# A decoder layer whose null key and null value leave the inner loop

What is changed: the null key is subtracted from the keys and the null value from the values when the weights are folded, and the first seven tiles' scores take two pairs of accumulator banks by turns, with both halves ahead of the transposes.

## The chip, the core and the metric

The kernel runs on one core of one Trainium2 chip. A core has five engines with queues of their own, which wait for each other by semaphores: TensorE (PE, matrix products, with its weight loads PEld), VectorE (DVE), ScalarE (ACT), GpSimd (POOL) and SyncE (SP, which starts the DMA transfers). PE writes into PSUM, eight banks of 128 partitions by 512 float32 words. The metric is the device time of one execution in microseconds (us), as a median of runs.

## The reference

x has 4 sequences of 1024 rows of 256; the context has 4 times 64 rows of 512. Three blocks, each after a layer norm and each with a residual: a gated recurrence, a cross attention of 16 heads of 64 with one null key and null value, and a feed-forward layer whose activations and weights are rounded to 8 bits and to three values. What matters here:

```
kv = einsum('bmc,cf->bmf', context, Wkv);  k, v = split(kv, 2), heads of 64
k = concatenate((nk, k), axis=-2)          # nk, nv: null_kv[0], null_kv[1], the same for each head
v = concatenate((nv, v), axis=-2)
sim = einsum('bhid,bhjd->bhij', q * DH**-0.5, k)     # 65 scores a head: 64 keys and the null key
attn = softmax(sim, axis=-1)
out = einsum('bhij,bhjd->bhid', attn, v)
out = einsum('bnf,fd->bnd', heads joined, Wout), then layer norm (ln_scale, ln_bias)
```

A softmax doesn't change when the same number is taken from all its scores, and its weights sum to one. So with k - nk as keys the null score is 0 for every row, and with v - nv as values the null value is a constant row added to each output.

## The kernel before

The work is in tiles of 128 rows, 32 in all, and the program is an order written out by hand for each engine, without a planner: what an engine does next is the next call in its function `stages2_3`.

Stage 1 runs the recurrence over eight groups of four tiles and ends about 97 us after the start. Its projections (L1286) multiply float32 operands split into a high and a low part (fp32r), 512 columns at a time.

The fold follows, until about 150 us. It multiplies Wq with the keys (`fold_keys`, L1374, into the maps Mhi and Mlo) and the values with Wout (`fold_values`, L1391, into VW), so that a tile needs only scores = normalised x times map, and output = probabilities times VW. `put_kvT` (ACT, L712) copies the projected context; `put_keys_hi` (ACT, L719) and `put_keys_lo` (DVE, L1030) write the maps' two parts; `put_values_first` (DVE, L1040) and `put_values_second` (ACT, L729) write VW. DVE also forms the null key's map column for each head (`null_key`) and lays the null value 16 times into a selection matrix (`null_values`, L1023), which PE multiplies with Wout in eight accumulating products of float32 (two passes each, L1401), half of them in front of the last `fold_values` and half in step 0.

Stages 2 and 3 are one loop over steps n from -2 to 31. Step n holds on PE: the scores of tile n+2 (`scores_half`, L1270), four groups of 4 heads with 4 x 65 = 260 columns in banks 0 to 3; the transposes of tile n's probabilities (L1510, L1518); the transpose of its null probabilities (L1524, to bank 7); gate and up of the feed-forward layer for tile n-5 (`gate_up`, also L1270; gate in banks 0 and 1, up in 2 and 3, which the scores use too); the output matmuls with VW (L1534, L1539: four float32 products each, two passes a product, so eight in the trace) and with the null values (L1540); in even steps the transposes of the activations of two coming tiles (`pair_T`, L1412); and down for tile n-7.

DVE in step n: `softmax_half` of tile n+2 for each half (maximum L1068, subtraction L1071), the low part of the transposed null probabilities (pTn, L1174), in odd steps xT2lo (L1046), the sum of exponentials of tile n+1 (L1080) and its reciprocal (L1085), gate times up (L1093), its largest value (L1100), the statistics of the output (L1198), the scales (L1132 qs, L1135 qr, L1136 zw, L1104 hw) and the residual (L1152). ACT copies the transposed probabilities (L822, L825, L827), applies silu (L768) and exp (L843), loading a table for each; POOL multiplies the exponentials by the reciprocals (`probabilities`: L554 for the keys, L557 for the null columns).

In steps 0 to 4 (`filling`) there is no gate and up. There the second half of the scores stands behind the transposes on PE, and behind the sum of exponentials and pTn on DVE. A half of the scores waits until the same half of the tile before has been subtracted (`sim_sub`), since all tiles use the same banks.

The functions, with the line numbers of the profile:

## Time and profile before

| | us |
|---|---|
| median of 3 runs | 513.25 |
| lowest, highest | 513.17, 515.15 |
| span of the profiled execution, first to last instruction | 510.8 |
| of it busy: PE, DVE | 476.4, 416.6 |
| of it busy: ACT, POOL | 334.4, 314.1 |

The profile shows one execution. Its own time is the span of 510.8 us, 2.4 less than the median of the runs, which also holds what lies before the first and behind the last instruction. The busy time of PE is a sum over matmuls that overlap each other: how far apart they start tells more than how long one lasts. A line number can be a helper's: L1270 is the helper `group`, under which scores, gate, up, down and the projections of the fold appear; the names of the operands (Mhi, Mlo; wgT; wuT; wdT) tell them apart. A few records of matmuls are missing from the trace, so that a group of four can read x3.

### The profile page before, as it was taken

How to read it: one execution, taken by the hardware profiler on the slowest of the kernel's cores; microseconds unless marked ns; L12 is line 12 of the kernel's file. 1: busy time of each engine (PE TensorE's matmuls, PEld its weight loads, DVE VectorE, ACT ScalarE, POOL GpSimd, SP SyncE). 2: the span in 40 equal slices, each digit the busy share in tenths (PEclk: the TensorE clock that was granted, in tenths of full speed). 3: DMA queues.
4: the chain of work that ended last, by engine and by line, in shares of the span. 5: the costliest groups of instructions: out<-in, count | busy, mean ns of one | idle time of the engine just before them, and what ended most of it. 6: DMA issues, size and time to landing. Idle time of an engine off the chain costs nothing.

```text
span 510.8 us, 8856 instructions
## 1 busy us (share of the span) xinstructions
PE 476.4 (93%) x2934; PEld 390.5 (76%) x2962; DVE 416.6 (82%) x933; ACT 334.4 (65%) x461; POOL 314.1 (61%) x486
## 2 busy tenths in 40 slices
PE   1999999999997998999999999999999999999774
PEld 0778888877676887888888888888888888887432
DVE  4789898968437558799999899898998998997786
ACT  3556652245333334788888888888897888787562
POOL 2234546510003457788787887887878778788861
PEclk9999999999999999999999999999999999999979
DMA  8996000320000000011122211313132212221234
GB/s 256 324 360 255 3 0 1 72 52 2 0 1 1 1 1 7 6 27 42 36 52 45 50 39 38 58 42 49 36 50 46 53 37 52 44 52 37 63 85 117
DMA packets 67116, 31.80 MB, mean 62 GB/s; under 512 B 49664, under 2 KB 65280, under 8 KB 67072
## 3 DMA queue, kind: packets, MB, share of 16 engines
q1 hardware_dynamic: 67072, 31.24, 24.5%
q8 instruction: 24, 0.39, 0.3%
q14 instruction: 20, 0.16, 0.1%
HBM read 15.24 MB, written 4.19 MB: 38 GB/s over the span
## 4 chain that ended last, share of the span: by engine, by line
PE 74%; DVE 11%; POOL 4%; DMA 3%; issue 3%; SPq 2%; ACT 2%; DVEq 0%; POOLq 0%; ACTq 0%
PE psum L1270 33%; PE psum L1534 10%; PE psum L1539 9%; PE psum L1286 9%; DMA xs<-in_x_dram 3%; PE psum L1510 2%; PE psum L1518 2%; SPq L397 2%; PE psum L1412 2%; PE psum L1391 1%; PE psum L1305 1%; DVE den L1080 1%; PE psum L1374 1%; DVE region_d L1071 1%; DVE mx L1068 1%
## 5 line engine op out<-in xcount | busy, mean ns | idle before, releaser
L554 POOL TENSOR_TENSOR region_d<-region_d,rden 128x1024 f32<-128x1024 f32 x32 | 60.9, 1903 | 74.9 <-DVE rden L1085 74.9
L1270 PE MATMUL psum<-Mhi,xT2hi 128*128 128x260 f32 x256 | 75.9, 297 | 0.2
L1270 PE MATMUL psum<-Mlo,xT2hi 128*128 128x260 f32 x256 | 72.9, 285 | 0.0
L1270 PE MATMUL psum<-Mhi,xT2lo 128*128 128x260 f32 x256 | 72.9, 285 | 0.0
L1534 PE MATMUL psum<-VW,region_d 128*128 128x256 f32 x256 | 61.2, 382 | 3.2 <-DVE pTn L1174 3.2
L1539 PE MATMUL psum<-VW,region_d 128*128 128x256 f32 x256 | 60.5, 379 | 0.0
L1534 PEld LDWEIGHTS psum<-VW,region_d 128*128 128x128 f32 x256 | 48.3, 191 | 13.1 <-DVE pTn L1174 4.5
L1068 DVE TENSOR_REDUCE mx<-psum 128x8 f32<-128x520 f32 x64 | 44.5, 696 | 13.0 <-PE psum L1270 11.4
L1539 PEld LDWEIGHTS psum<-VW,region_d 128*128 128x128 f32 x256 | 48.6, 190 | 6.6
L1093 DVE SCALAR_TENSOR_TENSOR region_c<-psum,zw,region_c 128x1024 f32<-128x1024 f32 x32 | 41.0, 1283 | 12.5 <-ACT region_c L768 10.9
L1270 PEld LDWEIGHTS psum<-Mhi,xT2hi 128*128 128x128 f32 x256 | 48.7, 190 | 1.3 <-issue 0.9
L1270 PEld LDWEIGHTS psum<-Mlo,xT2hi 128*128 128x128 f32 x256 | 48.9, 191 | 0.0
L1270 PEld LDWEIGHTS psum<-Mhi,xT2lo 128*128 128x128 f32 x256 | 48.8, 190 | 0.0
L1071 DVE TENSOR_TENSOR region_d<-psum,mx 128x520 f32<-128x520 f32 x64 | 44.8, 699 | 2.2
L843 ACT ACTIVATE region_d<-region_d 128x1040 f32<-128x1040 f32 x32 | 34.3, 1072 | 10.8 <-DVE region_d L1071 10.5
L516 POOL TENSOR_TENSOR pw_out<-pw_in,expo 128x8 f32<-128x8 f32 x8 | 13.2, 1647 | 43.7 <-DVE pw_in L912 43.7
L1100 DVE TENSOR_REDUCE amax<-region_c 128x1 f32<-128x1024 f32 x32 | 39.0, 1219 | 0.9
L1080 DVE TENSOR_REDUCE den<-region_d 128x16 f32<-128x1040 f32 x32 | 39.4, 1230 | 0.4
L768 ACT ACTIVATE region_c<-psum,zw 128x1024 f32<-128x1024 f32 x32 | 35.6, 1114 | 2.7 <-PE psum L1270 2.2
L780 ACT ACTIVATE region_c<-region_c,qr 128x1024 int16<-128x1024 f32 x31 | 35.3, 1139 | 2.8 <-DVE qr L1145 2.4
L571 POOL CAST region_d<-region_c 128x1024 bf16<-128x1024 int16 x31 | 32.2, 1038 | 4.8 <-ACT region_c L780 4.8
L822 ACT ACTIVATE region_d<-psum 128x512 f32<-128x512 f32 x32 | 19.1, 596 | 23.2 <-PE psum L1510 23.2
(151 smaller groups left out, 1217.5 us busy)
## 6 DMA issues: line engine op xcount, KB each, us to landing
out_dram<-xs SPq DMA_DIRECT2D x32, 128.0 KB, 1.9
xs<-in_x_dram SPq DMA_DIRECT2D x1, 2560.0 KB, 13.4
VW<-in_L_xattn_Wkv_dram SPq DMA_DIRECT2D x1, 2048.0 KB, 12.2
region_b<-in_L_xattn_Wkv_dram SPq DMA_DIRECT2D x1, 2048.0 KB, 18.4
xs<-in_x_dram SPq DMA_DIRECT2D x3, 512.0 KB, 7.4
region_w<-in_L_ffn_w_gate_dram SPq DMA_DIRECT2D x2, 512.0 KB, 10.3
region_w<-in_L_ffn_w_up_dram SPq DMA_DIRECT2D x2, 512.0 KB, 7.7
region_w<-in_L_ffn_w_down_dram SPq DMA_DIRECT2D x8, 128.0 KB, 5.1
```

The lines of the kernel that those rows point to most:

```text
L554: pool.tensor_tensor(p2[:, v, 0:H * MK].rearrange("p (h j) -> p h j", j=MK), e[:, :, 0:MK], rden[:, v, :].unsqueeze(2).broadcast_to([P, H, ...
L768: act.activation(hid3[v], banks(0, 2).rearrange("p b n -> p (b n)"), ACT.Silu, scale=zw[:, (n - 5) % 4, 0:1]).then_inc(silu_ready, 1)
L780: act.activation(nq3, hid3[t % 2], ACT.Copy, scale=qr[:, t % 2, 0:1]).then_inc(hq_done, 1)
L1068: dve.tensor_reduce(mx[:, hh, :].rearrange("p (b h) -> p b h", h=HB), scores, AX.X, ALU.max) \
L1071: dve.tensor_tensor(e2[:, u, hh * 2 * HB * J:(hh + 1) * 2 * HB * J].rearrange("p (b h j) -> p b h j", b=2, j=J), scores, mx[:, hh, :].rear ...
L1080: dve.tensor_reduce(den[:, :], e2[:, slot, :].rearrange("p (h j) -> p h j", j=J), AX.X, ALU.add) \
L1093: dve.scalar_tensor_tensor(out=hid3[v], in0=banks(2, 2).rearrange("p b n -> p (b n)"), scalar=zw[:, (n - 5) % 4, 1:2], in1=hid3[v], op0=AL ...
L1100: dve.tensor_reduce(amax[:, v, 0:1], hid3[v], AX.X, ALU.max, apply_absolute_value=True) \
L1270: mm = pe.matmul(dst, lhsT, rhs, start=i == 0, stop=i == len(terms) - 1)
L1286: mm = pe.matmul(bank(b), lhsT, rhs, start=i == 0, stop=i == len(terms) - 1)
L1534: pe.matmul(bank(7, D), pT[:, pair, :], VW[:, batch(n), pair, :], start=pair == 0, stop=False)
L1539: pe.matmul(bank(7, D), pT[:, pair, :], VW[:, batch(n), pair, :], start=False, stop=False)
```

## The change

The null key and value are loaded as two columns and negated once on POOL; `put_kvT` adds the negated column as a bias, so that maps and VW are made of k - nk and v - nv. The maps have 64 columns a head instead of 65, and a half of the scores is 8 heads of 64, one group of 512 columns in one bank. On DVE each half gets a third operation between maximum and subtraction: the shift -max(maximum, 0) of each head, written to the place of the null score in the row of exponentials (whose score is 0), and the subtraction becomes an addition of it. The transpose, the copy, the low part and the probabilities of the null columns go. The null value enters as one product of 33 rows (`ones_r` with `vnull`, the null value times Wout summed over the heads, in two parts), first in the output's accumulation; POOL sums Wout over its eight pieces for it, and DVE writes its low part in step 0 behind the second half of softmax of tile 2.

Scores of tile t lie in banks 2 (t % 2) and the next for t below 7, then always in 0 and 1; gate moves to banks 2 and 3, up to 0 and 1. In every step both halves stand ahead of the transposes, and each half of up waits for one half of softmax. The semaphores and buffers not shown are renamed or dropped to match.

```diff
@@ -362,9 +357,9 @@
-        def filling(n):
-            return isinstance(n, int) and 0 <= n < 5
+        def score_bank(t, hh):
+            return 2 * (t % 2) + hh if t < 7 else hh
@@ -524,14 +520,24 @@
+                    pool.wait_ge(null_loaded, 64)
+                    pool.tensor_scalar(nulls_neg[:, :], nulls[:, :], -1.0, 0.0, ALU.mult, ALU.add) \
+                        .then_inc(nulls_negated, 1)
...
+            pool.wait_ge(nvsel_zero, 1)
+            for row in (0, NR - 1):
+                pool.tensor_copy(nvsel[:, row:row + 1], nulls[:, 1:2]).then_inc(nv_set, 1)
+            pool.wait_ge(wout_loaded, 16)
...
-            pool.memset(nvsel, 0.0).then_inc(nvsel_zero, 1)
+            pool.tensor_tensor(wsum, wout[:, 0, :], wout[:, 1, :], ALU.add).then_inc(wout_summed, 1)
+            for pair in range(2, HC):
+                pool.wait_ge(wout_summed, pair - 1)
+                pool.tensor_tensor(wsum, wsum, wout[:, pair, :], ALU.add).then_inc(wout_summed, 1)
@@ -551,12 +557,8 @@
-                pool.tensor_tensor(p2[:, v, 0:H * MK].rearrange("p (h j) -> p h j", j=MK), e[:, :, 0:MK],
+                pool.tensor_tensor(p2[:, v, :].rearrange("p (h j) -> p h j", j=MK), e[:, :, 0:MK],
...
-                    .then_inc(p_ready, 1)
-                pool.tensor_tensor(p2[:, v, H * MK:].rearrange("p (m h) -> p m h", h=H),
-                                   e[:, :, MK].unsqueeze(1).broadcast_to([P, NP // H, H]),
-                                   rden[:, v, :].unsqueeze(1).broadcast_to([P, NP // H, H]), ALU.mult) \
@@ -709,13 +711,15 @@
-                act.activation(kvT[:, i % 4, :], bank(i % 2, BM), ACT.Copy).then_inc(kvT_ready, 1)
+                null = 0 if i < HC else 1
+                act.activation(kvT[:, i % 4, :], bank(i % 2, BM), ACT.Identity, bias=nulls_neg[:, null:null + 1]) \
+                    .then_inc(kvT_ready, 1)
...
-                    at = slot_of(2 * i + half_) * J
+                    at = slot_of(2 * i + half_) * MK
@@ -991,41 +993,10 @@
-            def null_key(k):
...
-                dve.tensor_scalar(hi, null, DH ** -0.5, None, ALU.mult).then_inc(mnull_hi, 1)
-                dve.scalar_tensor_tensor(out=lo, in0=null, scalar=DH ** -0.5, in1=hi.bitcast(F32), op0=ALU.mult,
-                                         op1=ALU.subtract).then_inc(mnull_put, 1)
-            def null_values():
-                for pair in range(HC):
-                    for j in range(2):
-                        rows = slice(j * DH, (j + 1) * DH)
-                        column = nvsel[rows, :].rearrange("p (c m h) -> p c m h", c=HC, h=H)[:, pair, 0::2, slot_of(2 * pair + j)]
-                        dve.tensor_copy(column, nv[rows, :].broadcast_to([DH, 3])).then_inc(nv_set, 1)
...
-                    at = slot_of(2 * i + half_) * J
+                    at = slot_of(2 * i + half_) * MK
@@ -1060,19 +1027,18 @@
-                scores = banks(2 * hh, 2)[:, :, 0:HB * J].rearrange("p b (h j) -> p b h j", j=J)
+                scores = bank(score_bank(n, hh)).rearrange("p (h j) -> p h j", j=MK)
+                e = e2[:, u, hh * HB * J:(hh + 1) * HB * J].rearrange("p (h j) -> p h j", j=J)
...
-                    if positive(2 * n - 2):
-                        dve.wait_ge(p_ready, 2 * n - 2)
-                dve.tensor_reduce(mx[:, hh, :].rearrange("p (b h) -> p b h", h=HB), scores, AX.X, ALU.max) \
-                    .then_inc(max_done, 1)
+                    if positive(n - 1):
+                        dve.wait_ge(p_ready, n - 1)
+                dve.tensor_reduce(mx[:, hh, :], scores, AX.X, ALU.max).then_inc(max_done, 1)
...
-                dve.tensor_tensor(
-                    e2[:, u, hh * 2 * HB * J:(hh + 1) * 2 * HB * J].rearrange("p (b h j) -> p b h j", b=2, j=J),
-                    scores,
-                    mx[:, hh, :].rearrange("p (b h) -> p b h", h=HB).unsqueeze(3).broadcast_to([P, 2, HB, J]),
-                    ALU.subtract).then_inc(sim_sub, 1)
+                dve.tensor_scalar(e[:, :, MK], mx[:, hh, :], 0.0, -1.0, ALU.max, ALU.mult).then_inc(shift_done, 1)
+                dve.wait_ge(shift_done, 2 * n + hh + 1)
+                dve.tensor_tensor(e[:, :, 0:MK], scores, e[:, :, MK].unsqueeze(2).broadcast_to([P, HB, MK]), ALU.add) \
+                    .then_inc(sim_sub, 1)
@@ -1161,20 +1127,12 @@
-                if exists(n + 2, T) and not filling(n):
+                if exists(n + 2, T):
...
-                    dve.wait_ge(vwn_hi, 1)
-                    lo = VWnull[4 * H:NP, :]
-                    dve.tensor_tensor(lo, psum[4 * H:NP, 7, 0:D], lo.bitcast(F32), ALU.subtract).then_inc(vwn_ready, 1)
-                if exists(n, T):
-                    dve.wait_ge(pTn_hi, n + 1)
-                    lo = pTn[2 * H:3 * H, :]
-                    dve.tensor_tensor(lo, psum[2 * H:3 * H, 7, D:D + P], lo.bitcast(F32), ALU.subtract) \
-                        .then_inc(pTn_ready, 1)
-                if filling(n):
-                    softmax_half(n + 2, 1, u)
+                    dve.wait_ge(vnull_hi, 1)
+                    lo = vnull[NR - 1:NR, :]
+                    dve.tensor_tensor(lo, psum[NR - 1:NR, 7, 0:D], lo.bitcast(F32), ALU.subtract).then_inc(vnull_ready, 1)
@@ -1394,13 +1352,11 @@
-            def null_values(first, end):
-                pe.wait_ge(nv_set, 2 * HC)
-                for pair in range(first, end):
-                    mm = pe.matmul(psum[0:NP, 7, 0:D], nvsel[:, pair * NP:(pair + 1) * NP], wout[:, pair, :],
-                                   start=pair == 0, stop=pair == HC - 1)
-                return mm
+            def null_values():
+                pe.wait_ge(nv_set, 2)
+                pe.wait_ge(wout_summed, HC - 1)
+                pe.matmul(psum[0:NR, 7, 0:D], nvsel[:, :], wsum, start=True, stop=True).then_inc(vnull_psum, 1)
@@ -1444,22 +1398,21 @@
-                if n == 0 and hh == 1:
+                if n == 1:
...
-                if positive(2 * n - 1 + hh):
+                if n >= 7:
...
+                elif n >= 2:
+                    pe.wait_ge(sim_sub, 2 * n - 3 + hh)
...
-                    pe.wait_ge((silu_ready, h_ready)[hh], n - 7)
-                for g in (2 * hh, 2 * hh + 1):
-                    mm = group(bank(g, HB * J),
-                               [(xT[:, (u4 // 2) % 2, k, (u4 % 2) * P:(u4 % 2 + 1) * P],
-                                 m[:, k, b, g * HB * J:(g + 1) * HB * J])
-                                for k in range(KD) for xT, m in ((xT2hi, Mhi), (xT2hi, Mlo), (xT2lo, Mhi))])
-                mm.then_inc(sim_psum, 1)
+                    pe.wait_ge(h_ready, n - 7)
+                group(bank(score_bank(n, hh)), [(xT[:, (u4 // 2) % 2, k, (u4 % 2) * P:(u4 % 2 + 1) * P],
+                                  m[:, k, b, hh * HB * MK:(hh + 1) * HB * MK])
+                                 for k in range(KD) for xT, m in ((xT2hi, Mhi), (xT2hi, Mlo), (xT2lo, Mhi))]) \
+                    .then_inc(sim_psum, 1)
...
@@ -1475,19 +1428,18 @@
-                pe.wait_ge(sim_sub, upto(2 * n + 5, 2 * T))
...
-                    mm = group(bank(j), [(nT3[:, slot, k, :], wgT[:, k, j * 512:(j + 1) * 512]) for k in range(KD)])
+                    mm = group(bank(2 + j), [(nT3[:, slot, k, :], wgT[:, k, j * 512:(j + 1) * 512]) for k in range(KD)])
...
-                pe.wait_ge(sim_sub, upto(2 * n + 6, 2 * T))
...
-                    mm = group(bank(2 + j), [(nT3[:, slot, k, :], wuT[:, k, j * 512:(j + 1) * 512]) for k in range(KD)])
+                    pe.wait_ge(sim_sub, upto(2 * n + 5 + j, 2 * T))
+                    mm = group(bank(j), [(nT3[:, slot, k, :], wuT[:, k, j * 512:(j + 1) * 512]) for k in range(KD)])
@@ -1496,14 +1448,13 @@
                     if n == 0:
-                        null_values(HC // 2, HC).then_inc(vwn_psum, 1)
-                    if not filling(n):
-                        scores_half(n + 2, 1, (u4 + 2) % 4, half(n + 2 - u), batch(n + 2))
+                        null_values()
+                    scores_half(n + 2, 1, (u4 + 2) % 4, half(n + 2 - u), batch(n + 2))
                 else:
...
-                    pe.wait_ge(p_ready, 2 * n + 2)
+                    pe.wait_ge(p_ready, n + 1)
                     if positive(n):
@@ -1517,27 +1468,25 @@
                     mm.then_inc(pT1_psum, 1)
+                if exists(n + 2, T) and exists(n - 5, T):
+                    gate_up(n, v)
+                if exists(n, T):
                     if positive(n):
...
                     if n == 0:
-                        pe.wait_ge(vwn_ready, 1)
-                    pe.transpose(psum[0:NP, 7, D:D + P], p2[:, u, H * MK:], ident[:, :]).then_inc(pTn_psum, 1)
-                if filling(n):
-                    scores_half(n + 2, 1, (u4 + 2) % 4, half(n + 2 - u), batch(n + 2))
-                if exists(n + 2, T) and exists(n - 5, T):
-                    gate_up(n, v)
-                if exists(n, T):
-                    pe.wait_ge(pTn_ready, n + 1)
+                        pe.wait_ge(vnull_ready, 1)
+                    pe.matmul(bank(7, D), ones_r[:, :], vnull[:, :], start=True, stop=False)
                     pe.wait_ge(pT0_ready, n + 1)
                     for pair in range(HC // 2):
-                        pe.matmul(bank(7, D), pT[:, pair, :], VW[:, batch(n), pair, :], start=pair == 0, stop=False)
+                        pe.matmul(bank(7, D), pT[:, pair, :], VW[:, batch(n), pair, :], start=False, stop=False)
                 if exists(n, T):
...
                     for pair in range(HC // 2, HC):
-                        pe.matmul(bank(7, D), pT[:, pair, :], VW[:, batch(n), pair, :], start=False, stop=False)
-                    pe.matmul(bank(7, D), pTn[:, :], VWnull[:, :], start=False, stop=True).then_inc(out_psum, 1)
+                        mm = pe.matmul(bank(7, D), pT[:, pair, :], VW[:, batch(n), pair, :], start=False,
+                                       stop=pair == HC - 1)
+                    mm.then_inc(out_psum, 1)
                 if u == 0 and exists(n, T - 4):
...
                 if exists(n - 7, T):
```

On DVE, the odd step of the steady part, before. mx holds the maxima, region_d the rows of exponentials (and xT2lo's source), and den the sums:

```order
L1068 TENSOR_REDUCE mx<-psum 128x8 [waits p_ready,sim_psum]
L1071 TENSOR_TENSOR region_d<-psum,mx 128x520 [waits max_done]
L1068 TENSOR_REDUCE mx<-psum 128x8 [waits sim_psum]
L1071 TENSOR_TENSOR region_d<-psum,mx 128x520 [waits max_done]
L1174 TENSOR_TENSOR pTn<-psum,pTn 16x128 [waits pTn_hi]
L1046 TENSOR_TENSOR xT2lo<-psum,xT2hi 128x512 [waits xT2_ready]
L1080 TENSOR_REDUCE den<-region_d 128x16 [waits exp_done]
```

The same place after:

```order
L1036 TENSOR_REDUCE mx<-psum 128x8 [waits p_ready,sim_psum]
L1038 TENSOR_SCALAR region_d<-mx 128x8 [waits max_done]
L1040 TENSOR_TENSOR region_d<-psum,region_d 128x8x64 [waits shift_done]
L1036 TENSOR_REDUCE mx<-psum 128x8 [waits sim_psum]
L1038 TENSOR_SCALAR region_d<-mx 128x8 [waits max_done]
L1040 TENSOR_TENSOR region_d<-psum,region_d 128x8x64 [waits shift_done]
L1017 TENSOR_TENSOR xT2lo<-psum,xT2hi 128x512 [waits xT2_ready]
L1046 TENSOR_REDUCE den<-region_d 128x16 [waits exp_done]
```

Two small operations have come in, each in a chain of waits, and the one on pTn has gone. The neighbours stand as they did.

On PE, a step among 0 to 4, before; the first row opens the first half of the scores, and the one that waits for sim_sub behind the null transpose (80x128) opens the second:

```order
L1270 MATMUL psum<-Mhi,xT2hi 128x260 [waits sim_sub,xT2_lo_ready]
...
L1510 MATMUL psum<-ident,region_d 128x128 [waits pT0_ready,p_ready]
L1510 MATMUL psum<-ident,region_d 128x128 x3
L1518 MATMUL psum<-ident,region_d 128x128 [waits pT1_ready]
L1518 MATMUL psum<-ident,region_d 128x128 x3
L1524 MATMUL psum<-ident,region_d 80x128 [waits y2_ready]
L1270 MATMUL psum<-Mhi,xT2hi 128x260 [waits sim_sub,xT2_lo_ready]
...
L1534 MATMUL psum<-VW,region_d 128x256 [waits pT0_ready,pTn_ready]
```

And after, from the start of the second half of the scores:

```order
L1228 MATMUL psum<-Mhi,xT2hi 128x512 [waits sim_sub,xT2_lo_ready]
...
L1461 MATMUL psum<-ident,region_d 128x128 [waits pT0_ready,p_ready]
L1461 MATMUL psum<-ident,region_d 128x128 x3
L1469 MATMUL psum<-ident,region_d 128x128 [waits pT1_ready]
L1469 MATMUL psum<-ident,region_d 128x128 x3
L1479 MATMUL psum<-vnull,ones_r 128x256 [waits y2_ready]
L1482 MATMUL psum<-VW,region_d 128x256 [waits pT0_ready]
```

The second half has moved in front of the transposes, where the wait for sim_sub is one for the tile two before. Between the transposes and VW nothing is left but the null product, and VW no longer waits for pTn.

## Rows read from the trace of the kernel before

**Rows 1.** The page: its span, and the chain that ended last, by engine.
```profile
span 510.8 us, 8856 instructions
...
PE 74%; DVE 11%; POOL 4%; DMA 3%; issue 3%; SPq 2%; ACT 2%; DVEq 0%; POOLq 0%; ACTq 0%
```

**Rows 2.** Chain in order of time: start, length (us), work; steady part.
```profile
241.19 1.73 PE psum L1534 x8
...
448.65 1.73 PE psum L1534 x8
```

**Rows 3.** Timeline of PE, steady step: start, length (us), line, operands, shape.
```profile
308.33 0.37 PE L1270 MATMUL psum<-Mhi,xT2hi 128*128 128x260 f32 x1
...
311.30 0.60 PE L1510 MATMUL psum<-ident,region_d 128*128 128x128 f32 x4
...
313.14 1.03 PE L1270 MATMUL psum<-wuT,region_d 128*128 128x512 bf16 x4
314.01 1.89 PE L1534 MATMUL psum<-VW,region_d 128*128 128x256 f32 x8
```

**Rows 4.** Timeline of DVE, the same step and the next; brackets: idle before.
```profile
310.06 0.70 DVE L1068 TENSOR_REDUCE mx<-psum 128x8 f32<-128x520 f32 x1 [0.51 <-PE psum L1270]
...
312.96 0.28 DVE L1174 TENSOR_TENSOR pTn<-psum,pTn 16x128 fp32r<-16x128 f32 x1
313.28 0.69 DVE L1046 TENSOR_TENSOR xT2lo<-psum,xT2hi 128x512 fp32r<-128x512 f32 x1
...
319.23 0.17 DVE L1132 TENSOR_SCALAR qs<-amax 128x2 f32<-128x2 f32 x1
319.43 0.17 DVE L1135 RECIPROCAL qr<-qs 128x2 f32<-128x2 f32 x1
319.51 0.21 DVE L1136 TENSOR_SCALAR zw<-wscale,qs 128x2 f32<-128x2 f32 x1
...
320.15 0.69 DVE L1068 TENSOR_REDUCE mx<-psum 128x8 f32<-128x520 f32 x1
...
325.86 1.28 DVE L1093 SCALAR_TENSOR_TENSOR region_c<-psum,zw,region_c 128x1024 f32<-128x1024 f32 x1 [0.73 <-ACT region_c L768]
```

**Rows 5.** Chain in order of time, steps 0 to 4.
```profile
167.32 1.82 PE psum L1534 x8
...
171.43 1.44 PE psum L1270 x12
174.33 1.15 DVE den L1080
...
202.20 1.99 PE psum L1534 x8
```

**Rows 6.** Timeline of PE, VW of step 1.
```profile
176.12 1.99 PE L1534 MATMUL psum<-VW,region_d 128*128 128x256 f32 x8 [0.66 <-DVE pTn L1174]
```

**Rows 7.** Chain, a stretch of the projections of stage 1.
```profile
38.82 4.12 PE psum L1286 x18
```

**Rows 8.** Timeline of PE, first and last fold of values.
```profile
131.61 1.96 PE L1391 MATMUL psum<-region_b 64*64 64x256 f32 x32 [1.17 <-DVE Mlo L1030]
...
148.66 1.96 PE L1391 MATMUL psum<-region_b 64*64 64x256 f32 x32
```

**Rows 9.** Timeline of ACT, in front of the last fold.
```profile
147.32 1.08 ACT L729 ACTIVATE VW<-psum 128x512 f32<-128x512 f32 x2
```

**Rows 10.** Timeline of POOL, its first work behind the fold.
```profile
158.56 1.90 POOL L554 TENSOR_TENSOR region_d<-region_d,rden 128x1024 f32<-128x1024 f32 x1 [50.72 <-DVE rden L1085]
```

**Rows 11.** Busy by window: length, PE, PEld, DVE, ACT, POOL; clock, DMA, GB/s.
```profile
164.00:165.00 1.00, 0.72 (x4) 0.72 (x5) 0.23 (x1) 0.24 (x2) 1.00 (x1) 0.50 0.00 0
```

**Rows 12.** Timeline of PE, the null transpose of step 0.
```profile
164.28 0.43 PE L1524 MATMUL psum<-ident,region_d 128*80 128x128 f32 x1 [2.32 <-DVE VWnull L1169]
```

**Rows 13.** Timeline of ACT, copy of the first four transposes, steady step.
```profile
311.94 0.60 ACT L822 ACTIVATE region_d<-psum 128x512 f32<-128x512 f32 x1 [0.76 <-PE psum L1510]
```

**Rows 14.** All executions of L1132: ns shortest/median/longest, first and last start.
```profile
L1132 DVE TENSOR_SCALAR qs<-amax x32: 153/169/172, 198.5 to 492.8; 128x2 f32<-128x2 f32 x26, 128x1 f32<-128x1 f32 x6
```

98 lines of the change are left out of this document (34 added, 64 removed).

## The prediction, made before the changed kernel ran

> **What bounds the kernel now.** I read the page first: the chain that ended last lies for 74% on PE and for 11% on DVE [rows 1]. Then the chain in order of time, which gives the pace: the matmuls of probabilities times VW start at 241.19 for one tile and at 448.65 twenty tiles later [rows 2], so a tile costs 10.37 us and a pair of tiles 20.75. Tiles go in pairs because an even step also transposes two coming tiles' activations on PE, and an odd step subtracts their rounded part on DVE (L1046).
>
> Next PE's timeline in one such step [rows 3]. From the scores at 308.33 to the transposes at 311.30 are 2.97 us; to up at 313.14 another 1.84, which are gate (as long as up, 0.87) and nine transposes of 0.108; up 0.87; then VW, twice 1.73. There is no hole: PE is full. DVE's timeline [rows 4] is nearly as full. From 310.06 to 320.15 it never waits, 10.09 us; in the next step it waits 0.73 us for the silu. So two limits stand side by side: PE's own work, and a loop through DVE: first maximum of the odd step, all its work up to the next step's first maximum, two halves of softmax, and then PE's up, VW and the rest until the next scores. A gain on PE is therefore not simply passed on.
>
> Before that come five steps without the feed-forward part, where no engine is full: VW starts at 167.32 and, four steps on, at 202.20 [rows 5], 8.72 us a step. There the order decides, and VW waits for DVE's pTn, 0.66 us at 176.12 [rows 6], which stands behind the sum of the exponentials (174.33 [rows 5]).
>
> **The change part by part.**
>
> *Scores, steady.* Before: 24 matmuls of 260 columns, 0.12 us apart (12 in 1.44 [rows 5]), 2.9 us and a start-up of 0.07. After: 12 of 512 columns. The nearest row has the same kind of operands in the first stage, 18 in 4.12 us [rows 7], 0.229 each, so 2.75. Bounds: 0.217, the pace of the four bf16 matmuls of 512 columns (313.14 to 314.01 [rows 3]), and 0.24, two of 260. I take 0.229: 0.17 us a tile less on PE. The null transpose goes too, 0.11. The null product of 80 rows is replaced by one of 33 rows with as many columns: even. PE alone then needs 20.75 - 2 x 0.28 = 20.2 us a pair.
>
> *DVE, steady.* Each half gains one tensor_scalar of 128x8 between maximum and subtraction, each waiting for the one before. Its nearest row is qs, a tensor_scalar of 128x2 with a dependent successor: 0.17 long, and 0.20 from its start (319.23) to the next start [rows 4]. So +0.40 a tile. The subtraction on pTn goes, 0.32 (312.96 to 313.28). 520 elements become 512, about 0.01 for each pass. Net +0.06 to 0.08 a tile. But of the stretch that up waits for, maximum to last subtraction, all 0.40 count: 2.90 (310.06 to 312.96) becomes 3.27. Bounds of one shift: 0.08, the distance of two small operations that don't wait for each other (qr and zw, 319.43 and 319.51), and 0.32, the place of pTn's subtraction. Eased is what up waits for: its second half alone needs the second half of softmax.
>
> *The loop.* First maximum of an odd step until that of the next: 10.09 + 0.40 - 0.32 = 10.17. Then 3.27 until the last subtraction. Then PE: the second half of up 0.43, null product 0.11, VW 3.46, transposes 0.43, down 0.87 (eight of 256 columns, as many as up's), in all 5.3; then 1.65 until the first half of the next scores has been written (before 310.06 - 308.33 = 1.73, by eleven gaps of 0.12 and a last matmul of 0.28; now five of 0.229 and a last one of some 0.4). Sum 20.4, and with about 0.1 for the restart of PE after a wait 20.5. That is above PE's 20.2, so the loop binds: 20.75 - 20.5 = 0.25 a pair. Eleven pairs (steps 8 to 29): **-2.8**.
>
> *Fold.* The 16 small copies of null_values on DVE go. PE waited 1.17 us in front of the first fold of values for the subtraction behind them [rows 8]; 0.1 of it I leave, since ACT's last copy for that fold may then be late: 1.05. The eight null passes of 0.216 before the last fold (148.66 [rows 8]) go from PE, but that fold also needs ACT's two copies from 147.32, 1.08 long [rows 9], done at 148.40: worth 0.15. The two null_key blocks on DVE never held PE up: nothing. POOL's seven new additions fall where it idled for 50.72 us until 158.56 [rows 10]: nothing; without that cover the null value's product would wait for them. Together -1.2: scores start at 149.4 (before 148.66 + 1.9 = 150.6).
>
> *First tiles.* PE now can write three tiles' scores in a row, so from 151.05 (149.4 + 1.65) DVE alone sets the pace: six halves of 1.64 (3.27/2), two sums with reciprocal of 1.45 (from 174.33 [rows 5] until pTn's 0.32 in front of VW at 176.12), 0.35 waiting for POOL's first probabilities (two tiles share the buffers), 0.42 for the low part of the null value, on which tile 0's output waits: 164.5. VW starts at 164.8 instead of 167.3. But the clock: from 164 to 165 PE had the granted clock 0.50 [rows 11], 1.2 GHz instead of 2.4, after a wait of 2.32 us for DVE [rows 12]. After the change PE waits longer there (160.3 to 164.5), and what follows is VW, the longest group. If the low clock lasts as long as before, some 3.4 us until VW's start, that costs 1.7 us. So tile 0 is done only **-0.9** earlier (2.5 less 1.7, fold included).
> [...]
>
> *Steps 1 to 4.* Both halves of the scores run ahead of the transposes (2.8), then 1.3 until ACT has copied the first four (0.64 from the transposes' start at 311.30 to the copy at 311.94, and 0.60 [rows 13]), null product and VW 3.57: 7.7 us, and 8.15 with two coming tiles' transposes, mean 7.9. DVE has 6 to 6.6 us of work in such a step and no longer stands in front of VW. 4 x (8.72 - 7.9) = **-3.3**.
>
> *Steps 5 to 7* begin the feed-forward part; DVE's extra work and PE's smaller 0.28 about cancel: **-0.1**. *Drain:* two steps in which pTn (0.3) is off DVE's path: **-0.6**; the rest is unchanged, gate and up only trade banks.
>
> **Sum.** -0.9 - 3.3 - 0.1 - 2.8 - 0.6 = -7.7 against the profiled execution's span of 510.8 [rows 1], so 503.1. The median of the runs lies 2.4 above that span: 505.5.
>
> **The rivals.**
> 1. *PE alone binds, the loop is shorter.* If a shift costs 0.12, the loop falls to 20.2 and so does a pair: 11 x 0.55 = 6.1 instead of 2.8: 502.2. For it: PE shows hardly a wait today. Against: 10.09 us of DVE without a hole.
> 2. *The steady part gives nothing.* A shift of 0.26 eats the 0.25 of a pair: 508.3. For it: a strided result, 65 elements apart, of which before shows no small one.
> 3. *The clock does not fall, or falls on nothing:* 1.7 less, 503.8.
> 4. *The change doesn't do in steps 1 to 4 what it says.* If scores ahead only push the transposes back, and VW starts no earlier (another wait, for y2 or the probabilities, in pTn's place), 3.3 are lost: 508.8. For it: no engine is full there, so waits decide. Against: what VW waits for by name is pTn [rows 6].
> 5. *Slower.* The shift stands in the loop four times a pair. Before it decides, the whole gain must be eaten: 4 x 11 x (x - 0.2) = 7.7, so x = 0.38 us. At 0.55 the kernel takes 505.5 + 15.4 = 521. It would need the shift to wait for POOL's running operation. Against it: qs, of the same kind, took 153 to 172 ns in all its 32 executions [rows 14].
> The Trainium skill (GPSIMD Engine Reference, Key points) has just this rule: POOL shares its SBUF interfaces with VectorE and contends with DVE instructions in a 2-port mode or with two SBUF inputs. By it the shift, with its one source and its result in SBUF, could be such an instruction, and this rival's 521 its price; the 32 executions of qs do not bear it out.
>
> **How the numbers follow.** Forecast 0.44, first rival 0.17, second 0.15, third 0.08, fourth 0.09, fifth 0.04, and 0.03 for something unseen near no change. The likeliest one's own range is 503.5 to 507.5. A shift at its upper bound, 0.32, gives 505.5 + 11 x 0.48 = 510.8, one at its lower and scores at 0.217 give PE's limit 20.0 a pair and 500.2. Over all cases I give 500.5 to 509.8. Under 0.5% (2.6 us) this kernel's measurement can't tell a difference: faster means below 510.7. Faster 0.87, same 0.08, slower 0.05.
>
> **What would show it.** In the profile after: score matmuls 0.229 apart; pairs of 20.5 us between VW starts, with PE waiting shortly for DVE's subtraction in front of the second half of up in every other step, and DVE without idle time from an odd step's first maximum to the next; shifts of 0.17, 0.20 apart from what follows; steps 1 to 4 of 7.7 and 8.15 us without a wait for DVE in front of VW; VW of tile 0 at 164.8 and a granted clock of 0.5 around it. Wrong, if DVE waits for PE in every step of the steady part (then rival 1), if shifts last over 0.25 (rival 2 or 5), or if the low clock spreads into steps 1 to 4.

## The result, and the profile after

The changed kernel takes **522.5 us** (median of 4 runs, 522.31 to 525.78) against 513.59 for the kernel before in the same session: ratio 1.0172, 95% interval 1.0139 to 1.0206. It is slower by 1.7%, where 505.5 us had been forecast. Two executions lie far outside the rest, 817.39 us for the kernel before beside the first group of runs and 1223.74 for the kernel with the null value early; no ratio counts them, and the latter kernel's median is 496.16 without it. The profiled execution:

```profile
span 520.7 us, 7943 instructions
...
PE 72%; DVE 14%; DMA 4%; SPq 3%; issue 2%; POOL 2%; ACT 2%; POOLq 0%; ACTq 0%; DVEq 0%
```

Against [rows 1], the share of DVE in the chain has gone up from 11 to 14%. Where the 9.9 us of span arose is seen best in the starts of the matmuls of probabilities times VW (PE's timeline; L1534 before, L1482 after), in us:

| step | 0 | 1 | 4 | 7 | 29 | 31 | end |
|---|---|---|---|---|---|---|---|
| before | 167.12 | 176.12 | 202.20 | 230.95 | 458.56 | 475.54 | 510.8 |
| after | 167.03 | 177.36 | 201.18 | 230.11 | 465.73 | 481.74 | 520.7 |
| after less before | -0.1 | +1.2 | -1.0 | -0.8 | +7.2 | +6.2 | +9.9 |

So the steady part (steps 7 to 29, eleven pairs) lost 8.0, the drain behind step 31 another 3.7, and the first steps gained 0.8 where 4.3 had been forecast. A steady pair takes 21.55 us in place of 20.75.

PE's timeline in an odd steady step, the one to hold against [rows 3]:

```profile
310.01 0.48 PE L1228 MATMUL psum<-Mhi,xT2hi 128*128 128x512 f32 x1
310.32 0.39 PE L1228 MATMUL psum<-Mlo,xT2hi 128*128 128x512 f32 x1
310.55 0.40 PE L1228 MATMUL psum<-Mhi,xT2lo 128*128 128x512 f32 x1
...
312.84 0.60 PE L1461 MATMUL psum<-ident,region_d 128*128 128x128 f32 x4
313.28 0.60 PE L1469 MATMUL psum<-ident,region_d 128*128 128x128 f32 x4
313.71 1.03 PE L1228 MATMUL psum<-wgT,region_d 128*128 128x512 bf16 x4
314.58 0.59 PE L1228 MATMUL psum<-wuT,region_d 128*128 128x512 bf16 x2
315.55 0.61 PE L1228 MATMUL psum<-wuT,region_d 128*128 128x512 bf16 x2 [0.38 <-DVE region_d L1040]
316.09 0.38 PE L1479 MATMUL psum<-vnull,ones_r 33*128 33x256 f32 x1
316.40 1.99 PE L1482 MATMUL psum<-VW,region_d 128*128 128x256 f32 x8
318.23 1.89 PE L1487 MATMUL psum<-VW,region_d 128*128 128x256 f32 x8
319.96 1.04 PE L1228 MATMUL psum<-wdT,region_d 128*128 128x256 bf16 x8
```

The scores take 2.83 us (2.97 before), the matmuls 0.23 apart as forecast but for 0.31 behind the first. The transposes take 0.87. Up now has a hole in its middle: its second half starts 0.97 behind its first and not 0.43, since PE waits for DVE's subtraction. Then the null product: from its start to down's are 3.87 us, where VW and the null product before took 3.57 (376.21 to 379.78 in the trace of before). That is 0.3 more for a part that I had called even.

DVE's shifts (L1038) in that step, and what POOL does then:

```profile
312.40 0.37 DVE L1038 TENSOR_SCALAR region_d<-mx 128x8 f32<-128x8 f32 x1
...
314.13 0.64 DVE L1038 TENSOR_SCALAR region_d<-mx 128x8 f32<-128x8 f32 x1
```
```profile
312.26 0.48 POOL L603 TENSOR_SCALAR region_d<-region_d,qr 128x256 f32<-128x256 f32 x1
...
314.01 0.73 POOL L549 TENSOR_TENSOR region_d<-region_d,lb_bc 128x256 f32<-128x256 f32 x1
```

The first shift ends at 312.77, POOL's instruction at 312.74; the second at 314.77 and POOL's at 314.74. That a running instruction of POOL keeps the shift from ending is called a hold in what follows. In the first steps it is POOL's probabilities, its longest instruction there:

```profile
158.10 1.50 DVE L1038 TENSOR_SCALAR region_d<-mx 128x8 f32<-128x8 f32 x1
```
```profile
157.67 1.91 POOL L560 TENSOR_TENSOR region_d<-region_d,rden 128x1024 f32<-128x1024 f32 x1 [44.58 <-DVE rden L1051]
```

All 64 shifts, put beside POOL's timeline: 36 began while such an instruction ran, one of them only 0.02 us behind its start, and all 36 ended 0.02 to 0.04 us after it. Four more began when less than 0.14 us of one was left, eight under POOL's instructions of 128x1 and sixteen beside nothing; these took 0.17 to 0.20. Four of the eight had over 0.3 us of a 128x1 power (0.57 long) still ahead of them. One of these four:

```profile
387.25 0.17 DVE L1038 TENSOR_SCALAR region_d<-mx 128x8 f32<-128x8 f32 x1
```
```profile
387.00 0.57 POOL L583 TENSOR_TENSOR sc<-sc,expo 128x1 f32<-128x1 f32 x1
```

In sum the 64 last 26.5 us, undisturbed they would last 64 x 0.175 = 11.2.

Tile 0, which answers to [rows 11, 12]:

```profile
166.53 0.58 PE L1479 MATMUL psum<-vnull,ones_r 33*128 33x256 f32 x1 [5.81 <-DVE vnull L1135]
167.03 3.78 PE L1482 MATMUL psum<-VW,region_d 128*128 128x256 f32 x8
```
```profile
164.00:165.00 1.00, 0.00 (x0) 0.00 (x0) 1.00 (x1) 0.00 (x0) 1.00 (x1) 0.91 0.00 0
165.00:171.00 6.00, 4.47 (x10) 3.48 (x11) 1.41 (x3) 0.00 (x0) 0.27 (x1) 0.50 0.01 3
171.00:172.00 1.00, 1.00 (x5) 0.82 (x4) 0.00 (x0) 0.00 (x0) 0.00 (x0) 0.67 0.00 0
```

PE waited 5.81 us in front of it. Within this wait, at about 164.8, its granted clock fell to 0.50 (1.2 GHz of 2.4) and stayed there until about 171.7: some 6.8 us, 5.1 of them with PE at work. Before, it was some 3.4 us (0.98 in 163 to 164, 0.50 until 167, 0.81 in 167 to 168), 3.1 of them at work.

### The profile page after: what moved, and what is told of

The parts are those of the page before. It is cut to its first block, busy times and chain, and to the rows that moved or that the text cites. A ratio compares the mean times of both kernels' runs of the same rounds, so it can differ in the third digit from the quotient of the medians.

```text
span 520.7 us, 7943 instructions
## 1 busy us (share of the span) xinstructions
PE 481.2 (92%) x2532; PEld 362.8 (70%) x2532; DVE 420.7 (81%) x939; ACT 329.3 (63%) x429; POOL 308.2 (59%) x465
## 4 chain that ended last, share of the span: by engine, by line
PE 72%; DVE 14%; DMA 4%; SPq 3%; issue 2%; POOL 2%; ACT 2%; POOLq 0%; ACTq 0%; DVEq 0%
PE psum L1228 30%; PE psum L1482 11%; PE psum L1487 10%; PE psum L1244 9%; DVE region_d L1040 4%; DVE mx L1036 3%; DVE region_d L1038 3%; DMA xs<-in_x_dram 3%; PE psum L1479 2%; SPq L392 2%; PE psum L1332 2%; PE psum L1461 2%; PE psum L1469 2%; PE psum L1349 1%; PE psum L1263 1%
## 5 line engine op out<-in xcount | busy, mean ns | idle before, releaser
L1482 PE MATMUL psum<-VW,region_d 128*128 128x256 f32 x256 | 65.6, 400 | 0.1
L1487 PE MATMUL psum<-VW,region_d 128*128 128x256 f32 x256 | 61.0, 381 | 0.0
L1036 DVE TENSOR_REDUCE mx<-psum 128x8 f32<-128x512 f32 x64 | 43.5, 680 | 14.2 <-PE psum L1228 14.2
L1482 PEld LDWEIGHTS psum<-VW,region_d 128*128 128x128 f32 x256 | 47.1, 194 | 9.7 <-ACT region_d L826 0.3
L1228 PE MATMUL psum<-Mhi,xT2hi 128*128 128x512 f32 x128 | 53.1, 415 | 0.3 <-DVE xT2lo L1017 0.3
L1228 PE MATMUL psum<-Mhi,xT2lo 128*128 128x512 f32 x128 | 50.3, 393 | 0.0
L1228 PE MATMUL psum<-Mlo,xT2hi 128*128 128x512 f32 x128 | 49.9, 390 | 0.0
L1040 DVE TENSOR_TENSOR region_d<-psum,region_d 128x512 f32<-128x512 f32 x64 | 44.3, 692 | 2.2
L1228 PE MATMUL psum<-wuT,region_d 128*128 128x512 bf16 x128 | 36.4, 381 | 3.6 <-DVE region_d L1040 3.4
L1228 PE MATMUL psum<-wgT,region_d 128*128 128x512 bf16 x128 | 33.7, 387 | 4.6 <-DMA region_d<-region_c 4.6
L784 ACT ACTIVATE region_c<-region_c,qr 128x1024 int16<-128x1024 f32 x31 | 35.3, 1140 | 3.4 <-DVE qr L1111 2.9
L1244 PE MATMUL psum<-xT1hi,w1hi 128*128 128x512 f32 x96 | 32.1, 416 | 1.9 <-ACT xT1hi L674 1.2
```

What stands on the lines that cost most here:

```text
L784: act.activation(nq3, hid3[t % 2], ACT.Copy, scale=qr[:, t % 2, 0:1]).then_inc(hq_done, 1)
L1036: dve.tensor_reduce(mx[:, hh, :], scores, AX.X, ALU.max).then_inc(max_done, 1)
L1040: dve.tensor_tensor(e[:, :, 0:MK], scores, e[:, :, MK].unsqueeze(2).broadcast_to([P, HB, MK]), ALU.add) \
L1228: mm = pe.matmul(dst, lhsT, rhs, start=i == 0, stop=i == len(terms) - 1)
L1244: mm = pe.matmul(bank(b), lhsT, rhs, start=i == 0, stop=i == len(terms) - 1)
L1482: pe.matmul(bank(7, D), pT[:, pair, :], VW[:, batch(n), pair, :], start=False, stop=False)
```

## The experiments

Four groups. Times are medians; each ratio is to the kernel before on the same chip.

**1. The shift, and the place of the null product.**

> The changed kernel with the null product behind the eight pairs of VW instead of ahead of them. Theory B (the null product ahead costs PE 0.3 us in every tile, and PE is what binds): 0.3 x 32 = 9.6 less, 513. Theory A (the shifts' hold on DVE binds, and the null product lies in the loop only once a pair): 0.3 x 12 = 3.6 less, 519. If its place is free: 522.5.

```
-  pe.matmul(bank(7, D), ones_r, vnull, start=True, stop=False)
   ... 16 matmuls of VW ...
+  pe.matmul(bank(7, D), ones_r, vnull, start=False, stop=True).then_inc(out_psum, 1)
```

522.43 us, ratio 1.0135 (1.0102 to 1.0168): nothing gained. A steady pair fell by 0.2 (21.36), and steps 1 to 4, where the product ahead lies beside the wait for ACT's copy, took 25.85 instead of 23.82. Theory B in this form (its place costs) falls. The 0.3 us are there in both places: with the product last, the stretch from VW's start to what follows it takes 3.86 us in an odd step, against 3.57 before.

> The changed kernel without the shift: the maximum is written negated into the null column by the reduction itself, and the subtraction adds it (the clamp of the maximum at zero is left out). Theory A: the hold of the shifts goes from the loop (a median of 0.37 us four times a pair), a pair falls from 21.5 to PE's own 20.7 with the null product ahead, and the first tile comes 2.5 us earlier: 11 x 0.85 + 1.5, so 511 to 512. Theory B alone: at most the 0.2 of an undisturbed shift counts, 519 or more.

```
-  dve.tensor_reduce(mx[:, hh, :], scores, AX.X, ALU.max)
-  dve.tensor_scalar(e[:, :, MK], mx[:, hh, :], 0.0, -1.0, ALU.max, ALU.mult)
+  dve.tensor_reduce(e[:, :, MK], scores, AX.X, ALU.max, negate=True)
```

This leaves out the clamp of the maximum at zero, as every kernel without the shift does here. 510.27 us, ratio 0.9898 (0.9855 to 0.9942): 12 us from this edit, as theory A has it.

> Both edits, no shift and the null product last. Both theories together: PE alone sets the pace, 20.2 us a pair by 20.7 less 0.5: 505 to 507, faster than the kernel before. If only one of the two mattered, this equals that one's time.

```
   the edits of the last two kernels together
```

511.72 us, ratio 0.9929 (0.9899 to 0.9959). The expected 505 to 507 was missed: without the shift PE binds at 20.7 to 20.8 us a pair, wherever the null product stands. So PE had gained nothing from the change, though its scores and transposes had become 0.25 a tile shorter. That opened the second question below.

> The changed kernel with the shift in the same place, of the same operands and with the same waits, but as a reduction over one element that writes the negated value, instead of a tensor_scalar (clamp at zero left out). Theory A with the form of the instruction as its cause: the hold by POOL is gone, the shift lasts 0.1 to 0.2 in all cases, and the kernel takes 514 to 517. Rival: POOL's work holds any DVE instruction that reads and writes SBUF, then its times spread from 0.17 to 1.5 as now and the kernel stays at 522.5.

```
-  dve.tensor_scalar(e[:, :, MK], mx[:, hh, :], 0.0, -1.0, ALU.max, ALU.mult)
+  dve.tensor_reduce(e[:, :, MK], mx[:, hh, :].unsqueeze(2), AX.X, ALU.max, negate=True)
```

512.04 us, ratio 0.9953 (0.9922 to 0.9984). One instruction in the same place, with the same operands and waits, but of another form (and without the clamp). All executions of L1038, first of the changed kernel, then of this one (ns shortest/median/longest):

```profile
L1038 DVE TENSOR_SCALAR region_d<-mx x64: 174/370/1500, 152.1 to 463.6; 128x8 f32<-128x8 f32 x64
```
```profile
L1038 DVE TENSOR_REDUCE region_d<-mx x64: 167/168/171, 152.6 to 454.2; 128x8 f32<-128x8 f32 x64
```

One of them under POOL's probabilities:

```profile
158.51 0.17 DVE L1038 TENSOR_REDUCE region_d<-mx 128x8 f32<-128x8 f32 x1
```
```profile
158.07 1.91 POOL L560 TENSOR_TENSOR region_d<-region_d,rden 128x1024 f32<-128x1024 f32 x1 [44.57 <-DVE rden L1051]
```

25 of the 64 reductions began with over 0.3 us left of an instruction of POOL larger than 128x1, and all of them took 0.17. So the form of the instruction decides, and 10 of the 17 us between forecast and result hang on it.

**2. The rows of the null product.** PE's weight loads in the changed kernel (the engine's second row in the profile; they normally run beside the matmul ahead):

```profile
315.55 0.11 PEld L1228 LDWEIGHTS psum<-wuT,region_d 128*128 128x128 bf16 x2 [0.87 <-DVE region_d L1040]
316.09 0.18 PEld L1479 LDWEIGHTS psum<-vnull,ones_r 33*128 33x128 f32 x1 [0.42 <-issue]
316.40 1.59 PEld L1482 LDWEIGHTS psum<-VW,region_d 128*128 128x128 f32 x8
```

The load of the 33-row product starts when up's last matmul is about through, and VW's first load (316.40) when the null product is. Both are bare, that is, no matmul runs beside them. Hence theory C: it is the number of rows.

> The changed kernel without the shift, and with the null product of 128 rows instead of 33 (the 95 new rows of the null value are zero, so nothing changes in what is computed). Theory C: a product of 33 rows between products of 128 costs PE 0.40 to 0.49 us instead of 0.11, since its weights are not loaded beside the matmul ahead. Then a pair falls from 20.8 to 20.2 us and the time by 12 x 0.6 and 0.3 for each of the first steps: 501 to 503. Rival D: the null product costs that much because vnull and ones_r are read where before had pTn, whatever the rows: no change, 510.

```
-  NR = DH // 2 + 1
+  LO, NR = DH // 2, 128          # the low part stays in row 32
```

500.25 us, ratio 0.9745 (0.9713 to 0.9778). A steady pair is 20.17. The same place of it, loads and matmuls:

```profile
324.31 0.75 PEld L1226 LDWEIGHTS psum<-wuT,region_d 128*128 128x128 bf16 x4
325.17 0.19 PEld L1477 LDWEIGHTS psum<-vnull,ones_r 128*128 128x128 f32 x1
325.39 1.60 PEld L1480 LDWEIGHTS psum<-VW,region_d 128*128 128x128 f32 x8
```
```profile
324.52 1.03 PE L1226 MATMUL psum<-wuT,region_d 128*128 128x512 bf16 x4
325.20 0.47 PE L1477 MATMUL psum<-vnull,ones_r 128*128 128x256 f32 x1
325.50 1.67 PE L1480 MATMUL psum<-VW,region_d 128*128 128x256 f32 x7
```

(A record of VW is missing there; the other steps show x8 and the same distance.) From up's start to VW's are 0.98 us, of which up is 0.87: the null product costs 0.11, what the forecast took. In the kernel with 33 rows and no wait it was 1.27 (380.90 to 382.17 with no shift): 0.40.

> The same with 80 rows, as many as the null product of the kernel before has. Theory C, since before showed 0.11 for it: as with 128 rows, 501 to 503. Rival D: 510.

```
-  LO, NR = DH // 2, 128
+  LO, NR = DH // 2, 80
```

501.33 us, ratio 0.976 (0.9727 to 0.9792); a pair 20.18.

> The same with 64 rows. If theory C holds and it is the number of 32-row strips that must be that of the neighbours (rounded up to two, three or four), 64 behaves like 33: 510. If only a count that is no multiple of 32 costs: like 128 rows, 501 to 503.

```
-  LO, NR = DH // 2, 128
+  LO, NR = DH // 2, 64
```

510.84 us, ratio 0.9936 (0.9916 to 0.9956); a pair 20.82.

> No shift, with the null product of 32 rows (high and low part in rows 31 and 0, the same sum). Theory C: anything that doesn't fill more than 64 rows is loaded apart from its neighbours, 510. Rival: only 33 to 64 rows are, and 32 load like 128: 500.

```
-  LO, NR = DH // 2, 128          # high part in row 0, low part in row 32
+  LO, NR = DH // 2, 32           # high part in row 31, low part in row 0
```

509.52 us, ratio 0.9909 (0.9874 to 0.9945); a pair 20.81. So 32, 33 and 64 rows cost one price, and 80 and 128 the other. The step lies between 64 and 80 rows; nothing in between was tried.

> The changed kernel as it is, shift included, with 128 rows in the null product. The DVE loop with the held shifts binds a pair at 21.55; the null product lies in that loop once a pair: 12 x 0.3 and 1 for the first steps, 517 to 519. If PE's 0.3 a tile counted in full beside the held shifts: 513.

```
-  NR = DH // 2 + 1
+  LO, NR = DH // 2, 128          # the shift stays as changed
```

506.21 us, ratio 0.9872 (0.9828 to 0.9917), less than both values expected: the held loop does not bind at 21.55, a pair is 20.17. The profiled execution is the longest of the four, 509.94, and its first scores start at 152.54, some 3 us later than in the others of the changed kernel and its variants. All its shifts:

```profile
L1038 DVE TENSOR_SCALAR region_d<-mx x64: 174/176/1497, 155.0 to 452.4; 128x8 f32<-128x8 f32 x64
```

The median is 176, the undisturbed length. 16 of the 64 last over 0.2 us, where 36 did with 33 rows, and in sum they last 18.6 us instead of 26.5: the order on both engines is the same, but with steps 0.3 us shorter most shifts no longer fall on what holds them. The two causes are not a sum:

| | 33 rows | 128 rows |
|---|---|---|
| shift as changed | 522.5 (1.0172) | 506.2 (0.9872) |
| no shift | 510.3 (0.9898) | 500.25 (0.9745) |

> Without the shift, 128 rows, and the null product last. With the rows right, its place is worth nothing in the steady part (PE has the same work); tile 0 needs the null value either way. 500 to 501. If the place has a price of its own beside the rows, over 1 us from the 500.25 of the kernel with it ahead.

```
   no shift, 128 rows, and the null product behind VW, as in the first experiment
```

502.96 us, ratio 0.977 (0.975 to 0.979), where 500 to 501 had been expected: 2.7 above the kernel with the product ahead, though the two ratios' intervals overlap. A pair is 20.17 as there. It starts tile 0 at 163.54 instead of 163.91 and is 0.4 behind by step 31 (462.26 against 461.89), lost in steps 1 to 4; the rest lies in the drain.

**3. Both causes in the kernel before, and the length of POOL's instruction.**

> The kernel before with its null product cut from 80 rows to 64 (the last 16 rows, the low part's, are left out of it). Theory C: the weights of the product are no longer loaded beside the matmul ahead, nor those of the next beside it, 0.3 a tile on a PE that is full: 514 + 30 x 0.3 = 521 to 524. Rival: the price belongs to ones_r and vnull in the changed kernel and not to the rows: 514.

```
-  pe.matmul(bank(7, D), pTn[:, :], VWnull[:, :], start=False, stop=True)
+  pe.matmul(bank(7, D), pTn[0:64, :], VWnull[0:64, :], start=False, stop=True)
```

It leaves the low part's last 16 rows out. 521.66 us, ratio 1.0131 (1.0108 to 1.0155), for less work. A pair went from 20.75 to 21.17. One of its loads:

```profile
374.34 0.18 PEld L1540 LDWEIGHTS psum<-VWnull,pTn 64*128 64x128 f32 x1 [0.33 <-issue]
```

> The kernel before with a tensor_scalar of 128x8 between each maximum and its subtraction, which only copies the maximum. Undisturbed (0.20 from its start to the next): at most 0.8 a pair less the 0.73 that DVE waits: 514 to 518. Theory A, held by POOL, whose two instructions for the probabilities run some 2.2 us a tile: a mean of 0.4 and a maximum of 1.5 or more, 520 to 528.

```
+  dve.tensor_scalar(mx_copy[:, hh, :], mx[:, hh, :], 1.0, 0.0, ALU.mult, ALU.add)
   dve.tensor_tensor(e2[...], scores, mx_copy[...], ALU.subtract)    # was mx
```

523.48 us, ratio 1.0163 (1.0145 to 1.0181). All its copies of the maximum:

```profile
L1073 DVE TENSOR_SCALAR mx_copy<-mx x64: 171/172/1486, 152.9 to 464.1; 128x8 f32<-128x8 f32 x64
```

23 of the 64 last over 0.2 us. So the hold needs nothing of the rest of the change, nor the strided result. Pairs are 21.0 in most of the steady part and 21.7 in three, and this shows a limit of the hold. In an odd step the first copy begins just behind the start of POOL's tensor_scalar of 128x256. In the three long pairs it begins 0.06 to 0.08 us behind it and is held; in seven others 0.03 to 0.05 behind it, and is not. One of each kind, DVE's row and then POOL's:

```profile
334.73 0.44 DVE L1073 TENSOR_SCALAR mx_copy<-mx 128x8 f32<-128x8 f32 x1
```
```profile
334.66 0.48 POOL L603 TENSOR_SCALAR region_d<-region_d,qr 128x256 f32<-128x256 f32 x1
```
```profile
313.72 0.17 DVE L1073 TENSOR_SCALAR mx_copy<-mx 128x8 f32<-128x8 f32 x1
```
```profile
313.68 0.48 POOL L603 TENSOR_SCALAR region_d<-region_d,qr 128x256 f32<-128x256 f32 x1
```

Why the early ones escape isn't shown; POOL's instruction is not longer for it.

> The changed kernel with POOL's probabilities of a tile as four instructions of 256 elements instead of one of 1024. Theory A (a shift is held until the instruction that runs on POOL has ended, 1.9 us for one of 1024, about 0.5 for one of 256): the longest shift falls from 1.50 to 0.7 or less, and the time to 514 to 518. Rival: it is held until POOL's whole work for the tile is done, or by something else: shifts up to 1.5 as before and 522 or, by four starts instead of one on POOL, more.

```
+  for c in range(4):       # heads 4c to 4c+3 of the probabilities
       pool.tensor_tensor(p2[...][:, hs, :], e[:, hs, 0:MK], rden[...], ALU.mult)
```

521.74 us, ratio 1.0133 (1.0115 to 1.0152). The mechanism came as expected, the time did not:

```profile
L1040 DVE TENSOR_SCALAR region_d<-mx x64: 174/360/760, 151.6 to 464.4; 128x8 f32<-128x8 f32 x64
```

The longest shift is halved: 0.76, now under an addition of 128x256, and 0.59 under one of the four pieces. Step 7 starts at 227.77 instead of 230.11. But in the steady part it is POOL's other instructions that hold the shifts, its four pieces take 2.33 us and not 1.90, and a pair is 21.82.

**4. The first steps.**

> No shift, 128 rows, but the scores of all tiles in one pair of banks, so that PE waits with a tile's first half for the last tile's subtraction. By the forecast the two pairs of banks were worth 0.9 at tile 0 and most of the 3.3 us of steps 1 to 4: 503 to 504. Rival: the order of the two halves ahead of the transposes does it alone, and the second pair is worth under 1 us: 500 to 501.

```
-  return 2 * (t % 2) + hh if t < 7 else hh
+  return hh
```

501.64 us, ratio 0.9764 (0.9732 to 0.9796). VW starts at 163.85, 173.49, 196.73 and 224.58 in steps 0, 1, 4 and 7; with two pairs of banks it is 163.91, 173.55, 196.79 and 224.67. In this kernel, without the shift and with 128 rows, the second pair brings nothing; the 1.3 us by which its profiled execution is longer lie behind step 31.

> No shift, 128 rows, and the null value's product, copy and low part one step earlier, so that the low part (0.42 on DVE) stands in front of tile 2's softmax and not behind it. In the kernel with 128 rows PE stood idle for 3.58 us before tile 0's output, waiting for it, and then ran at half clock. Theory: VW(0) starts when ACT has copied the first probabilities, 160.3 instead of 163.9, the clock stays high, and the whole kernel gains 3 to 5 us: 495.5 to 497.5. Rival: later steps are set by DVE's order, which the edit doesn't shorten, and the lead is given back: 499 to 500.5.

```
 PE:   if n == -1: null_values(); scores_half(n + 2, 0, ...)    # was n == 0, behind it
 ACT:  if n == -1: copy of vnull                                 # was n == 0
 DVE:  if n == 0: low part of vnull; softmax_half(n + 2, 0, u)   # was behind both halves
```

**496.39 us, ratio 0.9647 (0.9618 to 0.9676)**: the fastest kernel of this study, 3.5% below before.

> The kernel with the null value early once more, for its profile: PE without the wait of 3.58 us before tile 0's output, VW(0) at 160.3, the granted clock at 1.0 from there, and steps of 7.6 to 8.1 behind it.

```
   no edit against the last kernel
```

496.91 us in one execution. PE at tile 0, and its clock behind it:

```profile
159.85 0.66 PE L1459 MATMUL psum<-ident,region_d 128*128 128x128 f32 x4 [0.89 <-POOL region_d L560]
...
160.70 0.36 PE L1477 MATMUL psum<-vnull,ones_r 128*128 128x256 f32 x1
161.19 1.99 PE L1480 MATMUL psum<-VW,region_d 128*128 128x256 f32 x8
```
```profile
161.00:171.00 10.00, 9.74 (x50) 8.30 (x50) 7.70 (x14) 4.90 (x10) 6.19 (x8) 1.00 0.01 2
```

No wait for the null value, no fall of the clock: VW(0) comes at 161.19 (160.3 had been expected), 2.7 us earlier than with the null value late and VW(1) 4.3 earlier (169.22 against 173.55), and this lead is kept to step 31 (457.47 against 461.89). Of 4.3 us, 2.7 are the wait and 1.6 the clock: with the null value late the clock was 0.50 for some 3.4 us behind VW(0), and half of that is 1.7.

> The changed kernel, shift included, with 128 rows and the null value's work one step earlier. If the shift costs only what holds it (two holds of 1.5 us in the first steps, undisturbed later, as with 128 rows alone), it lies 3 to 6 us above the 496.4 of the same kernel without it: 500 to 502, and the whole gain of the early null value is there beside the shift, against 506.2.

```
+  dve.tensor_scalar(e[:, :, MK], mx[:, hh, :], 0.0, -1.0, ALU.max, ALU.mult)    # the shift again
```

498.94 us, ratio 0.9728 (0.9673 to 0.9782): below what was expected. With rows and wait mended the shift costs 2.5 us by the medians (4 by the ratios), where it cost 12 (14) in the changed kernel.

## Why the prediction was wrong, by its steps

**DVE, steady: "+0.40 a tile", bounds 0.08 to 0.32 for one shift.** Wrong in kind. A shift lasts 0.17 or, in most cases, as long as POOL's instruction still runs, up to 1.50: 0.41 on average. Its upper bound came from the nearest small instruction and left out a wait. The fifth rival had the right mechanism, at a chance of 0.04. That it also had the right time ("At 0.55 the kernel takes [...] 521") is luck: by its own formula the measured 0.41 gives some 515, and the null product makes up the rest. What kept it there were the 32 executions of qs [rows 14], and they were no test: 17 began with POOL idle and 14 under one of its 128x1 instructions, 11 of them just as it ended. Only one (481.15, 0.15 long, under the cast below) began under a larger one, and it has a single element. Two rows of before could have told; zw is of the same form, 0.21 long in its 31 other executions, and ended here with POOL's cast:

```profile
481.42 0.32 DVE L1136 TENSOR_SCALAR zw<-wscale,qs 128x2 f32<-128x2 f32 x1
```
```profile
480.69 1.04 POOL L571 CAST region_d<-region_c 128x1024 bf16<-128x1024 int16 x1
```

What tells is the longest time of every instruction of this form on DVE, beside POOL's timeline. 29 of the other executions of zw ran under a 128x1 power and were not held, as the four shifts.

The Trainium skill says it outright on a page that I had not used (SBUF — State Buffer, SBUF: two separate sides): the port pair of VectorE and GpSimd is an exclusive lock, and whoever has it keeps it for the whole instruction. These traces agree: ends 0.02 to 0.04 us behind POOL's, 36 times. By the Trainium skill (VectorE: DVE Perf Modes, Mode 2×_2P) the mode in which one fp32 tensor with source and result in SBUF takes both ports is for tensor_scalar and tensor_copy; that the reduction in the shift's place was never held fits this. Neither section has the exceptions seen here, POOL's 128x1 powers and the copies that began right behind POOL's tensor_scalar.

**"The null product of 80 rows is replaced by one of 33 rows with as many columns: even."** Wrong by 0.3 us a tile, and the costliest single step: mending it alone gives 506.2. That this is near the forecast's 505.5 is in part luck: its pairs are 0.3 shorter than forecast, and its first steps some 3 us behind. I had priced the matmul by its columns, and not the two weight loads at its sides. It sits on PE, which is full, in every step. With it mended a pair is 20.17, the 20.2 that the forecast gave PE alone (first rival); the loop of 20.5, which I had put above it, does not bind even with the shift in it, so that sum was 0.3 too high.
The Trainium skill (TensorE: Matmul & The Clock Gate, Part 3) says in its list of what overlaps that a weight load does so with a matmul only where their row groups differ, though it also names a background weight buffer that a load can go to. The traces differ from the list: loads of 80 and 128 rows overlapped with matmuls of 128 rows, and loads of 32 to 64 rows, which need only part of the rows, did not. The measurement decides.

**Tile 0: "-0.9".** VW(0) was due at 164.8 and came at 167.03. Two held shifts (158.10 and 163.87) add 2.6 us on DVE's way there. The low clock then lasted some 6.8 us and not 3.4: VW of step 1 comes 10.33 us behind VW(0), and 8.03 where the clock stays at 1.00 (null value early), so it costs 2.3 us and not 1.7. With 128 rows and no shift, where PE waits 3.58 us, it costs 1.6, as forecast; the term was right for the wait that I had foreseen and too small for the one that the holds made. With 128 rows and no shift VW(0) is at 163.9, a little better than forecast.

**Steps 1 to 4: "7.7 us, and 8.15".** Right from step 1 on, where the starts are 8.17, 8.04 and 7.61 apart. But the first of the four steps took 10.33, mostly for the low clock, so that the four gained 0.9 and not 3.3. That the second pair of banks makes this possible, as the text has it ("PE now can write three tiles' scores in a row"), is not so: it brings nothing. What does was not undone by itself; the order of the halves, pTn's absence or both remain.

**Fold: "-1.2".** Scores start at 149.7, forecast 149.4 (149.1 to 150.2 in nearly all profiles of the variants). ACT's copies with a bias take 0.47 instead of 0.38; whether they are the 0.3 isn't shown.

**Drain: "-0.6".** Steps 30 and 31 gained 1.0, but what follows step 31 took 39.0 us instead of 35.3. In the profiles here it lies between 35.3 and 39.1, without regard to the edits, and the longer ones have a low clock at the very end. First before, then after:

```profile
505.00:510.00 5.00, 2.33 (x21) 1.49 (x18) 1.39 (x3) 0.60 (x1) 0.00 (x0) 1.00 0.23 79
```
```profile
515.00:521.00 6.00, 2.20 (x10) 1.02 (x8) 0.97 (x2) 0.00 (x0) 0.00 (x0) 0.50 0.13 44
```

What sets it stays open; it is up to 3.8 us that no term of mine held.

**The sum.** Against the forecast's span of 503.1, the 17.6 us are 3.5 in the first steps, 10.8 in the steady part and 3.3 behind it. The range ended at 509.8, which is even below the 510.8 that the prediction itself gives for a shift at its upper bound. Both bounds that made it rested on durations alone: neither a wait for POOL's instruction nor a bare weight load was in them.
